# Self-attention's output bias added to x ahead of time on GpSimd, and the router's input of the last two batches made in another order

## What is computed

```python
x = x + _L0_xattn_ref(_layernorm(x), ctx_1024, ...)
x = x + _L0_attn_ref(_layernorm(x), Wq, bq, Wk, bk, Wv, bv, Wo, bo)   # returns out @ Wo.T + bo
x = x + _L0_ffn_ref(_layernorm(x), ln_gamma, ln_beta, gate_w, w1, w2)

# in _L0_ffn_ref, xf being its input
rn = (xf - mu) * jax.lax.rsqrt(var + EPS) * ln_gamma + ln_beta
logits = rn @ gate_w.T
probs = jax.nn.softmax(logits, axis=-1)
rw, sel = jax.lax.top_k(probs, K)
```

## Time and profile before

| | |
|---|---|
| time, median of 3 runs | 989.26 us (987.99 to 994.92) |
| the profiled execution | 998.53 us, its span 996.6 us |
| PE busy | 904.5 us (91%) |
| DVE busy | 681.9 us (68%) |
| ACT busy | 529.5 us (53%) |
| POOL busy | 386.5 us (39%) |
| mean granted TensorE clock | 0.961 of full |

### The profile page before, as it was taken

One profiled execution on the slowest core, in us unless ns is written; L12 is line 12 of the kernel. 1 busy time (PEld: TensorE's weight loads), 2 busy tenths in 40 slices (PEclk: granted clock), 3 DMA queues, 4 the chain that ended last, 5 costly groups with the idle time before them and its releaser, 6 DMA issues. The chain is left out here.

```text
span 996.6 us, 24592 instructions
## 1 busy us (share of the span) xinstructions
PE 904.5 (91%) x10413; PEld 608.5 (61%) x10413; DVE 681.9 (68%) x1024; ACT 529.5 (53%) x813; POOL 386.5 (39%) x290
## 2 busy tenths in 40 slices
PE   5988999999999899999899999988786489999996
PEld 2463775766765766756667757753444377666673
DVE  7764687656677655678656556565678667998893
ACT  3642444564354464444455544450566347999893
POOL 2130666345566345556435545533220141112112
PEclk9997999999999999999999999997887689999998
DMA  9362121342121241220332211307403727999983
GB/s 337 105 174 68 34 65 41 110 143 72 46 63 30 89 145 42 66 48 24 102 116 79 66 30 37 88 1 297 148 2 115 272 86 269 402 404 401 403 339 43
DMA packets 48456, 134.64 MB, mean 135 GB/s; under 512 B 9870, under 2 KB 11790, under 8 KB 44506
## 3 DMA queue, kind: packets, MB, share of 16 engines
q1 hardware_dynamic: 45356, 126.78, 37.5%
q0 software_dynamic: 2800, 6.04, 2.9%
q10 hardware_dynamic: 192, 0.26, 0.1%
HBM read 94.99 MB, written 11.33 MB: 107 GB/s over the span
## 5 line engine op out<-in xcount | busy, mean ns | idle before, releaser
L455 POOL TENSOR_TENSOR acc_pool<-acc_pool,pT 128x1024 f32<-128x1024 f32 x90 | 211.7, 2353 | 154.9 <-ACT pT L719 153.3
L719 ACT ACTIVATE pT<-ps_s 128x1024 f32<-128x1024 f32 x124 | 126.8, 1022 | 212.8 <-PE ps_s L881 212.8
L561 DVE TENSOR_REDUCE mpart<-ps_b 128x1 f32<-128x512 f32 x256 | 173.8, 686 | 91.2 <-PE ps_b L859 90.2
L843 PE MATMUL ps_a<-wv_hi,cT_hi 128*128 128x128 f16 x1024 | 184.3, 220 | 0.4 <-ACT kbias L636 0.4
L845 PE MATMUL ps_a<-wv_hi,cT_lo 128*128 128x128 f16 x1024 | 183.2, 219 | 0.0
L844 PE MATMUL ps_a<-wv_lo,cT_hi 128*128 128x128 f16 x1024 | 183.1, 219 | 0.0
L556 DVE TENSOR_TENSOR k_lo<-k_f,k_hi 128x512 f16<-128x512 f32 x64 | 72.3, 1129 | 69.9 <-ACT k_hi L692 69.9
L843 PEld LDWEIGHTS ps_a<-wv_hi,cT_hi 128*128 128x128 f16 x1024 | 99.8, 97 | 11.8 <-issue 11.3
L859 PE MATMUL ps_b<-k_stack,q_stack 98*128 98x512 f16 x256 | 96.8, 384 | 8.2 <-DMA k_stack<-k_lo 5.3
L844 PEld LDWEIGHTS ps_a<-wv_lo,cT_hi 128*128 128x128 f16 x1024 | 100.3, 98 | 5.3
L845 PEld LDWEIGHTS ps_a<-wv_hi,cT_lo 128*128 128x128 f16 x1024 | 99.8, 97 | 0.0
(11 more groups left out here) (259 smaller groups left out, 1862.4 us busy)
## 6 DMA issues: line engine op xcount, KB each, us to landing
w_raw<-in_w SPq DMA_DIRECT2D x30, 2048.0 KB, 16.3
raw<-in_context SPq DMA_DIRECT2D x16, 1024.0 KB, 6.0
k_stack<-k_hi SPq DMA_DIRECT2D x252, 64.0 KB, 2.0
k_stack<-k_lo SPq DMA_DIRECT2D x128, 64.0 KB, 2.0
slots_in<-a_zeros SPq DMA_DIRECT2D x1, 3855.0 KB, 12.8
rows_in<-slots_in SPq DMA_DIRECT2D x15, 257.0 KB, 16.5
q_stack<-k_stack SPq DMA_DIRECT2D x12, 128.0 KB, 2.3
x_sb<-in_x SPq DMA_DIRECT2D x2, 512.0 KB, 4.5
```

The lines of the kernel that those rows point to most:

```text
L455: nc.gpsimd.tensor_tensor(acc_pool[:, :], pT[:, 0, :] if p == 1 else acc_pool[:, :], pT[:, p % PT, :], ALU.add).then_inc(pool_add, 1)
L561: nc.vector.tensor_reduce(mpart[:, j, kb:kb + 1], bank_at(step)[:, :], AX.X, ALU.max).then_inc(p1_max, 1)
L719: nc.scalar.activation(pT[:, p % PT, :], scores(w, p)[:, :], ACT.Exp, scale=SM_SCALE).then_inc(exp_done, 1)
L843: nc.tensor.matmul(to, cT_hi[:, c, keys], t.wv_hi[:, c, col], start=(c == 0), stop=False)
```

## The change

**The bias.** In step 0 GpSimd adds the output bias `bias[3]` to all four batches of x, after its rotary products and after the last `normalise` has read x. The output then needs one VectorE instruction for each batch, which scales the PSUM bank and adds x, where there were two (`a_y`, then `x_sb`). The tile `y` goes; `x_done` frees the PSUM bank, and `bo_added` is waited for.

**Batch 2 of the router.** In the tail step, `am_hat` is made before `m_normed_x` and both before `a_oT_lo`; PE's transposes wait for the first of the two alone.

**Batch 3 of the router.** Its four transposes go to two PSUM banks. ScalarE scales two chunks and VectorE the other two. All four `rows_low` of VectorE stand behind that, in front of the logits.

```diff
--- before.py
+++ after.py
@@ -971,7 +971,6 @@
...
         oT_hi, oT_lo = sb("a_oT_hi", [P, NG, P], F16), sb("a_oT_lo", [P, NG, P], F16)
-        y = sb("a_y", [P, D])
...
@@ -989,7 +988,7 @@
         scored, maxed, exped, inv, scaled = sem("a_scored"), sem("a_maxed"), sem("a_exped"), sem("a_inv"), sem("a_scaled")
         p_tr, p_out_act, p_out_dve = sem("a_p_tr"), sem("a_p_out_act"), sem("a_p_out_dve")
         o_mm, o_hi, o_lo = sem("a_o_mm"), sem("a_o_hi"), sem("a_o_lo")
-        y_mm, y_out, x_done = sem("a_y_mm"), sem("a_y_out"), sem("a_x_done")
+        y_mm, bo_added, x_done = sem("a_y_mm"), sem("a_bo_added"), sem("a_x_done")
 
         m_st, m_var, m_powed, m_normed = s.m_st, s.m_var, s.m_powed, s.m_normed
         zeroed = sem("a_zeroed")
@@ -1038,7 +1037,7 @@
             if d is not None:
                 ring += [("mg", d, g_out, d + 1)]
             if c is not None:
-                ring += [("y", c, y_out, c + 1)]
+                ring += [("y", c, x_done, c + 1)]
             if d is not None:
                 ring += [("gate", d, logits_out, d + 1)]
         place = {user[:2]: n for n, user in enumerate(ring)}
@@ -1104,6 +1103,13 @@
                         nc.gpsimd.tensor_tensor(dst[:, :, here], src[:, :, there], sines,
                                                 ALU.mult).then_inc(rot_done, 1)
                         pool.wait_ge(rot_done, 2 * n + half + 1)
+                if step == 0:
+
+                    pool.wait_ge(misc_in, 16 * 2)
+                    pool.wait_ge(normed, NB)
+                    for n in range(NB):
+                        nc.gpsimd.tensor_tensor(t.x[:, n, :], t.x[:, n, :], bias[3], ALU.add).then_inc(bo_added, 1)
+                    pool.wait_ge(bo_added, NB)
                 if c is not None and c + 1 < NB:
                     mixture_deviations(nc, pool, t, s, c, m_mv, m_rstd)
 
@@ -1204,6 +1210,8 @@
                         v.wait_ge(p_tr, 4 * c + n + 1)
                         nc.vector.tensor_copy(probT[:, HPG * n:HPG * (n + 1), :], ps_t[n % 2][:, :, :]).then_inc(p_out_dve, 1)
                 if d is not None and tail(step):
+                    v.wait_ge(g_tr, d)
+                    mixture_normalise(m_hat[:, :], d, 1)
                     mixture_input(d)
                 if a is not None:
                     rope_out(0, a)
@@ -1213,7 +1221,7 @@
                     nc.vector.scalar_tensor_tensor(out=oT_lo[:, :, :], in0=bank("o", c)[:, :].rearrange("p (g n) -> p g n", g=NG),
                                                    scalar=A_SCALE, in1=oT_hi[:, :, :], op0=ALU.mult,
                                                    op1=ALU.subtract).then_inc(o_lo, 1)
-                if d is not None:
+                if d is not None and not tail(step):
                     if d:
                         v.wait_ge(g_tr, d)
                     mixture_normalise(m_hat[:, :], d, 1)
@@ -1228,10 +1236,9 @@
                 split_low(step, "y")
                 if c is not None:
                     v.wait_ge(y_mm, c + 1)
-                    nc.vector.scalar_tensor_tensor(out=y[:, :], in0=bank("y", c)[:, :], scalar=UNSCALE,
-                                                   in1=bias[3], op0=ALU.mult, op1=ALU.add).then_inc(y_out, 1)
-                    v.wait_ge(y_out, c + 1)
-                    nc.vector.tensor_tensor(t.x[:, c, :], t.x[:, c, :], y[:, :], ALU.add).then_inc(x_done, 1)
+                    v.wait_ge(bo_added, c + 1)
+                    nc.vector.scalar_tensor_tensor(out=t.x[:, c, :], in0=bank("y", c)[:, :], scalar=UNSCALE,
+                                                   in1=t.x[:, c, :], op0=ALU.mult, op1=ALU.add).then_inc(x_done, 1)
                     if c + 1 < NB:
                         v.wait_ge(x_done, c + 1)
                         mixture_variance(c)
@@ -1384,7 +1391,7 @@
                         pe.wait_ge(normed, a + 2)
                         transposes("x", a + 1, hat[:, a + 1, :]).then_inc(tr, 1)
                 if d is not None:
-                    pe.wait_ge(m_normed, 2 * d + 2)
+                    pe.wait_ge(m_normed, 2 * d + (1 if tail(step) else 2))
                     transposes("mg", d, m_hat[:, :]).then_inc(g_tr, 1)
                 if c is not None:
                     to = free_bank("y", c)
@@ -1589,12 +1596,17 @@
                 nc.vector.scalar_tensor_tensor(out=n_lo[:, b, :], in0=t.normed[:, b, 0:D], scalar=A_SCALE,
                                                in1=n_hi[:, b, :], op0=ALU.mult, op1=ALU.subtract)
 
-            rows_low(0)
             v.wait_ge(powed, 3 * NB)
             for k, dst in ((1, hat[:, :]), (0, t.normed[:, last_b, 0:D])):
                 nc.vector.tensor_scalar(dst, t.x[:, last_b, :], mv[:, 0:1], rstd[:, k:k + 1],
                                         ALU.subtract, ALU.mult).then_inc(normed, 1)
-            for b in range(1, NB):
+
+            v.wait_ge(g_tr, NB)
+            for c in range(NC // 2, NC):
+                last = nc.vector.tensor_scalar(gT[:, c, :], ps_x[0][:, P * c:P * (c + 1)], affine[:, 0, c:c + 1],
+                                               affine[:, 1, c:c + 1], ALU.mult, ALU.add)
+            last.then_inc(g_out, 1)
+            for b in range(NB):
                 rows_low(b)
 
             v.wait_ge(g_mm, NB)
@@ -1756,7 +1768,7 @@
             for b in range(EARLIER):
                 rows_high(b)
             act.wait_ge(g_tr, NB)
-            for c in range(NC):
+            for c in range(NC // 2):
                 last = nc.scalar.activation(gT[:, c, :], ps_x[1][:, P * c:P * (c + 1)], ACT.Identity,
                                             bias=affine[:, 1, c:c + 1], scale=affine[:, 0, c:c + 1])
             last.then_inc(g_out, 1)
@@ -1798,8 +1810,10 @@
                 return last
 
             pe.wait_ge(normed, 2 * EARLIER + 1)
-            transposes(ps_x[1], hat[:, :]).then_inc(g_tr, 1)
-            pe.wait_ge(g_out, NB)
+            for c in range(NC):
+                last = nc.tensor.transpose(ps_x[1 - c // 2][:, P * c:P * (c + 1)], hat[:, P * c:P * (c + 1)], t.ident[:, :])
+            last.then_inc(g_tr, 1)
+            pe.wait_ge(g_out, NB + 1)
             for c in range(NC):
                 last = nc.tensor.matmul(ps_g[:, :], gT[:, c, :], gate[:, c, :], start=(c == 0), stop=(c == NC - 1))
             last.then_inc(g_mm, 1)
```

## The result

The changed kernel takes 988.9 us in the median of 20 runs (985.52 to 1172.29; one run of them stands apart, at 1172 us with a granted clock of 0.743, and is left out of the comparison). The kernel before, run beside it, has a median of 993.41 us in 20 runs (987.99 to 997.75). The ratio is 0.9964, with a 95% interval of 0.9948 to 0.9981: 3.6 us less, 1.9 to 5.2. (The quotient of the two medians is 0.9955, 4.5 us less; the document goes by the ratio, which stands on record with its interval.) The profiled execution took 985.89 us with a span of 984.1, 12.5 us less than the span before. Most of the excess over 3.6 goes with TensorE's clock, as the last part works out.

What follows compares the result with a forecast made beforehand. Bound: the wait chain from batch 3's statistics through the router into the expert-weight stream, with VectorE pacing late self-attention. 2.16 + 1.35 + 0.5 + 0.45 = 4.46 us saved, 1.1 lost, 3.4 net: 989.26 to 985.9 us, range 980.5 to 990.5.

Steps and rivals of the forecast that it cites:

- I take the difference over to the median: Base of the forecast time: profiled execution at 998.53 us, 9.3 above the median 989.26, from which 3.4 was taken.
- the terms: Savings of 2.16, 1.35, 0.5 and 0.45 us in self-attention and router, less 1.1 lost in step 0: 3.4 net.
- The bias on VectorE (2.16 us): Self-attention outputs of batches 0, 1 and 2: one VectorE instruction less each, 3 x 0.72 us saved.
- The rival that ACT or PE would end the waits: Steps 3 to 5: the bias's 2.16 us fall away, 1.2 us saved, 988.1 us; chance 0.12.
- Batch 2 of the router (1.35 us): Step 5: PE's output projection starts at the end of `a_oT_lo`, no longer behind `am_hat`'s transposes, 1.35 us sooner.
- Batch 3's output (0.5 us): Last output: VectorE's sum of 0.72 us goes, some 0.5 left since the logits' copy waits for batch 2's router matmuls.
- Batch 3 of the router (0.45 us): Mixture's start: router's matmul 0.76 us sooner by split scaling, logits only 0.45 sooner behind four low parts.
- The lock in step 0 (1.1 us lost): GpSimd's addition holds up VectorE's rotary sum of k through shared ports; 1.1 us lost, passed on through PE.
- The coin: Whether GpSimd's addition or VectorE's rotary sum starts first in step 0; VectorE first costs nothing, 984.8 us, chance 0.22.
- The clock: Rival: shorter PE gaps keep self-attention stretches at full clock, 2.9 us saved, another 2 from the tail; 981 to 983, 0.19.
- The slower rival: PE's gap ahead of step 1 grows to 2.8 us, low clock in steps 1 and 2 costs 6.9: 992.8 us, 0.07.
- A microsecond ahead of the stream is one at the end: Weight stream can't start before the router is done; a microsecond saved ahead of 830 us comes off the total.

Runs made afterwards that it cites:

- e4: Changed kernel with GpSimd's four additions waiting until VectorE's rotary sum of k in step 0 is done; 986.23 us, ratio 0.994 to the kernel before.
- e5: Changed kernel with 45 more copies of the logits on VectorE, delaying the router; 995.73 us, ratio 1.0032 to the kernel before.
- e8: Changed kernel with two small loads of constants issued at the start of self-attention, not of the mixture; 987.0 us, ratio 0.995 to the kernel before.
- e1: Kernel before with the bias part alone: four additions on GpSimd in step 0, one VectorE instruction per output; 988.98 us, ratio 0.996.
- e7: Changed kernel with 41 unread transposes in PE's waits in the router of batch 3; 984.39 us, ratio 0.9918 to the kernel before.
- e6: Kernel of e4 with batch 0's low part back ahead of the wait for GpSimd, three behind the scaled chunks; 985.32 us, ratio 0.9918 to the kernel before.
- e9: Changed kernel with additions behind the rotary sum, constants early, batch 0's low part between normalised input and scaled chunks; 984.82 us, ratio 0.9936 to the kernel before.
- e10: Kernel of e9 with 59 unread transposes in PE's waits in the router, 38 in the long wait; 984.09 us, ratio 0.9915 to the kernel before.
- e11: Kernel of e9 with 45 more copies of the logits on VectorE; 993.71 us, ratio 1.0006 to the kernel before.

## Why the prediction was right or wrong, by its own steps

**The time.** The forecast was 3.4 us less than before; the ratio gives 3.6, inside an interval of 1.9 to 5.2. The number 985.9 is 3.0 us under the measured 988.9 all the same. The step that failed is the base, where the prediction says "I take the difference over to the median": it did so to 989.26, a median of three runs. In 20 runs, those three among them, the kernel before has 993.41, so that 4.2 us of the forecast time were never there. Against that base the 985.9 reads as 7.5 us of gain, and the measured one is 3.6 by the ratio and 4.5 by the medians.

That 3.4 and 3.6 stand so near each other is in part luck. The interval is 3.3 us wide; the terms as the time lines have them come to 3.7 to 3.9; and how much of them reaches the end is known to within some us only.

**The bias on VectorE (2.16 us).** Right. Between the same instructions of the two time lines, VectorE came 0.71, 0.73 and 0.73 us sooner behind the outputs of batches 0, 1 and 2. PE's gaps behind them shrank from 2.36 to 1.64 us, from 1.09 to 0.37 (its wait for batch 1's logits in step 4) and from 1.04 to 0.47, and each still names VectorE. The rival that ACT or PE would end the waits didn't come.

**Batch 2 of the router (1.35 us).** Right: the projection starts behind `a_oT_lo` and not behind `am_hat`, the weight pieces end before it, and with that edit alone step 5 was 2.0 us shorter, part of it by the clock (2.9 us fewer at the low level).

**Batch 3's output (0.5 us).** Right: from the start of its last VectorE instruction on x to the statistics it is 1.27 us (775.00 to 776.27), against 1.82 before from the first of the two (783.97 to 785.79): 0.55.

**Batch 3 of the router (0.45 us).** Mis-sized as a whole: 0.94 us from the statistics to the logits, 0.74 in e4, e5 and e8. The step that I had counted gave 0.42, from the start of the scaling to the logits (3.47 to 3.05), with VectorE's two chunks at 0.73 us in place of 0.58 and still inside ACT's 0.81. What I had left out lies ahead of it: the low part of batch 0 had held up GpSimd, 0.55 us in place of 0.19, and the normalised input now began 0.34 us sooner behind the statistics. The last 0.18 is PE's transposes, at a higher clock in this one execution.

**The lock in step 0 (1.1 us lost).** Right for the stall, with its cause shown: GpSimd's addition began at 687.20, VectorE's sum ended 1.80 us later, at 689.00, and with the additions behind it the sum was back at 0.69 (e4). The coin fell to GpSimd in all five executions profiled without that wait (e1, e5, e7, e8 and the changed kernel), with 1.78 us each time and GpSimd 0.02 to 0.03 us ahead. That the 1.1 us "goes through", as the prediction says, isn't shown: without the stall the profiled self-attention was longer, by what the clock did (see below).

**The clock.** I had it as a rival with 0.19, worth 2.9 to 5 us. In the profiled execution it came in full, and with it the prediction's own sign of being wrong, that the stretches of low clock move by more than the terms. Over all 13 profiled executions of this study, the length of self-attention less the terms above goes with the time at the low level. The kernel before has 40.4 us of it, and its length is what the others are held against. With 37.5 us at the low level self-attention was 0.7 us shorter than the terms alone make it, with 34.0 1.9, with 30.0 3.5, with 27.1 3.9 and with 20.5 6.8: each microsecond at the low level costs about a third of one there. So of the 9.4 us by which the profiled self-attention became shorter, 2.9 are the terms, and the 6.5 that they leave go with the clock. This is a relation over executions and not an experiment on the clock.

Over many runs little of that stays. The mean clock of the changed kernel is 0.962 over 19 runs, that of the kernel before 0.960 over 33, and 0.963 and 0.961 in two further sets of 20 and 29. The pair of profiled executions was an unlucky one of the one (998.53, above all of its 20 runs shown) and a lucky one of the other (985.89, third lowest). The slower rival, by the longer gap ahead of step 1, is refuted for what was profiled: behind a gap of 2.79 us the clock was as it had been, and better from step 2 on.

The profiled executions hold one thing more that isn't explained. The four of the changed kernel with the stall in step 0 (the changed kernel itself, e5, e7 and e8) all had 20.4 to 20.6 us at the low level and 102.2 to 102.8 us of self-attention. The five with the additions behind the rotary sum (e4, e6, e9, e10 and e11) all had 27.1 to 34.1 and 104.2 to 106.7. So the longer gap went with the better clock, and in these traces with more than it had cost. It can't be the gap alone, since e1, with the stall and the old order of step 5, had 30.0. The times over many runs don't bear this out: e4 and e9 are not slower than the changed kernel, and their mean clocks are 0.963 and 0.965. Chance among nine executions is one reading; an effect of the gap on the clock is another, and no run here decides between them.

**A microsecond ahead of the stream is one at the end.** Likely for most of it, by a delay and not by a gain: 6.8 of 9.2 and 7.0 to 8.9 of 9.0 us, each give or take 3. From the start of the picking to the end the executions took 190.6 to 198.1 us, whatever the router did; 20.0 to 25.8 us of it went by until the scattered rows had landed. Where the missing part goes isn't settled; that VectorE's splits release a weight load in the chain after the change, and not the queue behind the scatter, is one place where it could. The prediction's sign of being wrong here, a stream that begins no earlier, did not come.

## What to carry to other kernels

Take the base from as many runs as the gain asks for: with runs that spread over 10 us, three of them set a median that was 4 us off, more than the change was worth. When work moves to GpSimd, or moves on VectorE beside GpSimd, look for instructions of VectorE with two inputs in SBUF at the moment where GpSimd starts; one wait more on GpSimd (it stood 0.97 us in e4), or another place for the instruction, takes the stall away. Whether that shortens the whole is a second question, which one profiled execution can't answer while the clock moves by more. And when a step comes sooner, look at the small loads that were issued late because nobody waited for them: in e4, e6 and e7 VectorE stood 0.9, 0.7 and 2.5 us for one, though that issuing it early helps (e8) isn't shown.

## What the runs showed of the hardware that I had not expected

The hold-up works in both directions and on tiny instructions: a low part of 128x512 on VectorE made an addition of 128x1 on GpSimd last 0.55 us in place of 0.19, in four executions against nine.

Time and mean clock of single runs go together: in 19 runs of the changed kernel each 0.01 of clock is 4.6 us, with a correlation of -0.81. The clock also fell once, in e10, from the full to the low level at about 785.9 while PE was busy, after 2.70 us of work in the 5 us up to 785. It came back at about 789.3 with PE doing nothing but the unread transposes.
